# Graph attention and routed experts: normalising ahead of a mask conversion, and a score row made from a projection column

## The chip, the cores and the metric

The kernel runs on one core of a Trainium2 chip, in one launch. The metric is the device time of an execution in microseconds (us), as the median of several runs. The engines are named as the profile names them: PE is TensorE (PEld its weight load), DVE is VectorE, ACT is ScalarE, POOL is GpSimd, SP is SyncE, which here only issues transfers.

## The reference

```
x = x + gat(layernorm(x), adj)              # x is 4096 x 128, adj 4096 x 4096 of 0 and 1
x = x + ffn(layernorm(x))                   # eight experts, the best two for each row

gat(h, adj):  Wh = h @ W + b
              e[i, j] = leaky_relu(Wh[i] . a1 + Wh[j] . a2, 0.2), -9e15 where adj[i, j] is 0
              softmax over j, then attention @ Wh
ffn(x):       gate = x @ Wg.T + bg; top 2, softmax over the two
              out = sum over the two of p * (relu(x @ W1[e].T + b1[e]) @ W2[e].T + b2[e])
```

## The kernel before

Nodes are cut into 32 tiles of 128, and the tiles into 8 row groups of four (GT = 4). Attention is worked off in five stages of destination tiles, WB = [8, 8, 8, 6, 2], and each stage runs over all 32 source tiles. So there are 160 steps; step n = 32 g + u handles source tile u for stage g.

In a step, VectorE's `weigh(n)` (line 971) builds the weights of one source tile for all destinations of the stage, from three things: a row over destinations `c_bc` (128 equal partitions, one value for each destination), a column over sources `E_col`, and the mask `G`. It takes the larger of row and column and the smaller of that and the mask. TensorE's `attend(n)` (line 1600) multiplies `Wh` of the source tile with these weights and adds up in the two accumulators `acc`. The mask comes as int32 from DRAM in chunks of two steps (SP, `load_chunk`, line 531) and is converted to bf16 by ScalarE (`edges`, line 1355). At the end of a stage ScalarE's `evacuate` (line 1386) copies both accumulators to `numT`, and the rest of the stage's work (division, second layer norm, gate, routing) is spread over the steps of the next stage. The experts' tiles run between later steps and after them.

Each engine follows an order written out by hand: a loop over steps n in which each piece of work has its step, with ScalarE starting its conversions 6 steps ahead, VectorE its weights 4 steps ahead, and SP its loads 12 steps ahead. Engines wait for each other only by semaphores. `group_at(n, part, first)` says which row group i has its turn at step n: group i comes at n = 4 (i - 2) + part. `weigh` may be five steps ahead of `attend`, for there are six buffers `prob`.

The first stage also prepares the row groups i = 0 to 7. VectorE takes mean and variance (`stats`), GpSimd raises to the power -1/2 and makes the bias (`pow_group`, its last operation in line 702), ScalarE normalises four tiles (`normalise`, line 1320; groups 0 and 1 on VectorE), TensorE transposes them (`transposes`, line 1545), ScalarE copies the result out of PSUM (`keep_hT`, line 1329), TensorE projects them on the nine columns of `wag` (`project`, line 1558: the source score and eight gate columns), and ScalarE makes the column values (`keep_E`, lines 1336 and 1337). For the destinations' row, TensorE multiplies a matrix that holds the vector a1 in each column with the transposed group, a product of 512 columns (`project_s`, line 1567), and ScalarE takes the exponential into `c_bc` (`keep_s`, line 1347). Groups 0 to 3 have this in stage 0; groups 4 to 7 in stage 1, at steps 48, 50, 52 and 54 (`row_at`). VectorE cuts the row of each next stage off at 1 (`group_row`, line 940).

There is a second branch (`general`) for scores of a wide reach, which is not taken with these inputs.

Of the kernel before, what the change touches and what calls it, by code (L numbers as in the profile page):

```python
# [5 lines left out]
def build(nc, x, adjT, W, Wb, a, WgT, bg, wcat, wlast, b2, out):  # L6
    fp32, fp16, bf16 = mybir.dt.float32, mybir.dt.float16, mybir.dt.bfloat16
    i32, u32 = mybir.dt.int32, mybir.dt.uint32
    ALU = mybir.AluOpType
# [19 lines left out]
    GC = 1 + E  # L29
    TW = FW + E + 1  # L30
# [98 lines left out]
    with ctx:  # L129
# [10 lines left out]
        ybuf = nc.dram_tensor("ybuf", (2 * N, F), fp32).ap()  # L140

# [23 lines left out]
        def cut(base, *dims):  # L165
# [25 lines left out]
        wag = sb("wag", [P, GC])  # L191
# [34 lines left out]
            .rearrange("p (e f) -> p e f", f=F)  # L226
        rden = sb("rden", [P, SB])
# [79 lines left out]
        def row_at(n):  # L307

            i, r = divmod(n - TILES - 16, 2)
            return GT + i if r == 0 and 0 <= i < GROUPS - GT else None  # L310
# [13 lines left out]
        def score_row(i, late):  # L324

            return yt[:, i % 2, :] if late else acc[1][:, :] if i == 1 else m1[:, :]
# [13 lines left out]
        def projected_col(tiles, c):  # L340

            return pj[:, 0:TILES * GC].rearrange("p (u c) -> p u c", c=GC)[:, tiles, c]

# [42 lines left out]
        s_cg = sem("s_cg")  # L386
# [121 lines left out]
        def _(sp):  # L508
# [41 lines left out]

            rows, places = {}, {}
# [297 lines left out]
        def _(dve):  # L849
# [39 lines left out]
            def keep_Wh(i, general):  # L889
                tiles = slice(GT * i, GT * (i + 1))  # L890
                dve.wait_ge(s_ED, i + 1)
                if general:
                    nc.vector.tensor_copy(t_col[:, tiles], projected_col(tiles, 0))
# [17 lines left out]
            nc.vector.tensor_copy(wag[:, 0:1], wa[:, 1:2])  # L911
# [5 lines left out]
            nc.vector.tensor_tensor(wag[:, 1:GC], WgT_sb[:, :], wglast_bc[:, :], ALU.subtract).then_inc(s_wag, 1)  # L917
# [322 lines left out]
            def main(general):  # L1240
                for n in range(-LB, NS):
# [3 lines left out]
                    if not general:  # L1245
# [6 lines left out]
                        if n >= 0 and n % TILES == TILES - 8 and n // TILES + 1 < SG:  # L1252
                            group_row(n // TILES + 1)
# [6 lines left out]
                    if n == 26:  # L1260
# [3 lines left out]
                        nc.vector.tensor_tensor(xg[:, :, :], pj[:, 0:TILES * GC].rearrange("p (u c) -> p u c", c=GC)[:, :, 1:GC],  # L1264
# [51 lines left out]
        def _(act):  # L1316
# [7 lines left out]
            def keep_hT(i):  # L1324
                act.wait_ge(s_t0, i + 1)
                if i < GT:
                    ge(act, s_sm, i - 1)
# [4 lines left out]
            def keep_E(i):  # L1332
                tiles = slice(GT * i, GT * (i + 1))
                act.wait_ge(s_wh, i + 1)
                t = projected_col(tiles, 0)
# [4 lines left out]
            def keep_s(i, general):  # L1340
                act.wait_ge(s_sm, i + 1)
                row = score_row(i, i >= GT and not general)
# [180 lines left out]
            with act.Else():  # L1523
                keep_s(0, True)
                keep_s(1, True)
                for i in range(GROUPS):
                    if i >= 2:
                        keep_hT(i)
# [7 lines left out]
        def _(pe):  # L1536
# [11 lines left out]
            def project(i, general=False):  # L1548
# [7 lines left out]
                for b in range(GT):  # L1556
                    at = (GT * i + b) * GC
                    last = nc.tensor.matmul(pj[:, at:at + GC], hT_of(i)[:, b * P:(b + 1) * P], wag[:, :],  # L1558
# [3 lines left out]
            def project_s(i, late=False):  # L1562
# [271 lines left out]
```

## Time and profile before

| what | value |
| --- | --- |
| median of 3 runs | 413.72 us (413.57 to 413.85) |
| the profiled execution | 413.95 us, span 412.2 us |
| mean granted TensorE clock | 0.989 of full speed |
| PE busy | 383.2 us, 93% of the span |
| DVE busy | 295.3 us, 72% |
| ACT busy | 270.1 us, 66% |
| POOL busy | 204.3 us, 50% |
| attention products (line 1600) | 236.0 us of PE in 576 records, two for each f32 product |
| row products (line 1567) | 16 records, 6 in bank m, 2 in acc, 8 in yt |

The span goes from the first to the last instruction of the profiled execution; its own time is 1.75 us longer. Busy times of PE are modelled from pipelined records. Times of other engines are durations of their instructions.

### The profile page before, as it was taken

The numbers are of one execution on the slowest core, as the hardware profiler recorded it, in microseconds if no ns is written. First come the engines' busy times: TensorE is split into PE (matmuls) and PEld (weight loads), VectorE is DVE, ScalarE is ACT, GpSimd is POOL, SyncE is SP. The second block draws the span as 40 slices with busy tenths as digits, with TensorE's granted clock in tenths as the row PEclk, the third lists the DMA queues.
The fourth block names the chain that finished last, engine by engine and source line by source line (L and its number), as shares of the span: only waits on it lengthen the run. The fifth ranks groups of instructions, "written<-read, shape, count | busy, mean of one in ns | idle before, by whom it ended". The sixth has DMA issues, their size and how long they took to land.

```text
span 412.2 us, 8417 instructions
## 1 busy us (share of the span) xinstructions
PE 383.2 (93%) x2434; PEld 257.1 (62%) x2434; DVE 295.3 (72%) x819; ACT 270.1 (66%) x451; POOL 204.3 (50%) x247
## 2 busy tenths in 40 slices
PE   1899999999999999999999999999989999999960
PEld 1545555444444444444366667798879999999960
DVE  5998896989799979899988696268951692111173
ACT  1589879675878666892376975458646666676630
POOL 3283451100401874206763058789787777555560
PEclk9999999999999999999999999999999999999995
DMA  6999998969959999898676994576577777667795
GB/s 197 358 425 373 344 353 251 422 250 374 384 220 305 354 302 408 322 319 328 185 244 236 380 316 145 184 245 219 191 231 237 251 239 240 218 222 240 243 361 184
DMA packets 45610, 116.44 MB, mean 282 GB/s; under 512 B 7517, under 2 KB 19682, under 8 KB 38902
## 3 DMA queue, kind: packets, MB, share of 16 engines
q1 hardware_dynamic: 37062, 100.02, 68.0%
q0 software_dynamic: 4320, 8.47, 6.2%
q10 hardware_dynamic: 4176, 7.34, 5.9%
q8 instruction: 23, 0.38, 0.4%
q14 instruction: 29, 0.24, 0.2%
HBM read 84.57 MB, written 13.07 MB: 237 GB/s over the span
## 4 chain that ended last, share of the span: by engine, by line
PE 75%; DMA 8%; DVE 6%; issue 4%; SPq 3%; ACT 2%; POOL 2%; ACTq 0%; POOLq 0%; DVEq 0%
PE acc L1600 46%; PE acc L1702 10%; DMA adj<-adjT 3%; PE hps L1684 3%; PE hps L1686 3%; PE hps L1685 3%; PE yt L1702 3%; DVE prob L971 2%; PE yt L1645 2%; DMA ybuf<-wst,dest 1%; DMA adj<-ybuf 1%; PE pj L1721 1%; PE pj L1558 1%; SPq L547 1%; PE yt L1567 1%
## 5 line engine op out<-in xcount | busy, mean ns | idle before, releaser
L1600 PE MATMUL acc<-prob,Wh 128*128 128x512 f32 (+1 forms) x576 | 236.0, 550 | 3.8 <-DVE prob L971 2.7
L971 DVE SCALAR_TENSOR_TENSOR prob<-s_bc,E_col,G_all 128x1024 f32<-128x1024 f32 (+2 forms) x159 | 169.7, 1096 | 21.9 <-PE acc L1600 18.5
L1600 PEld LDWEIGHTS acc<-prob,Wh 128*128 128x128 f32 x576 | 103.5, 190 | 98.8 <-issue 84.2
L1355 ACT ACTIVATE G_all<-adj 128x2048 bf16<-128x2048 int32 (+1 forms) x67 | 119.0, 1800 | 22.7 <-DMA adj<-adjT 12.8
L784 POOL DMA_INDIRECT xbuf<-xr,slot x64 | 72.6, 1135 | 49.6 <-PE acc L1600 30.5
L800 POOL DMA_INDIRECT ybuf<-wst,dest x71 | 73.2, 1031 | 45.4 <-ACT wst L1438 25.0
L1702 PE MATMUL acc<-wall,prob 128*128 x368 | 51.1, 282 | 0.0
L1702 PEld LDWEIGHTS acc<-wall,prob 128*128 128x128 f32 x368 | 44.7, 192 | 0.2
L1223 DVE COPY share<-slab 128x1 f32<-128x1 f32 x45 | 6.8, 155 | 47.1 <-DMA slab<-xbuf 44.5
L1428 ACT ACTIVATE prob<-hps 128x512 f32<-128x512 f32 x46 | 27.6, 599 | 6.5 <-PE hps L1686 1.4
L1438 ACT ACTIVATE wst<-acc,share 128x128 f32<-128x128 f32 x45 | 16.6, 368 | 17.3 <-PE acc L1702 15.6
L708 POOL TENSOR_TENSOR wst<-wst,wlb 127x512 f32<-127x512 f32 x8 | 13.5, 1685 | 28.2 <-DMA wlb<-wlast 28.2
L766 POOL TENSOR_TENSOR rstd<-ve,mhalf 128x8 f32<-128x8 f32 x3 | 5.0, 1660 | 45.2 <-DVE ve L1073 45.2
L1702 PE MATMUL yt<-wall,wst 128*128 x192 | 26.8, 282 | 0.0
L1702 PEld LDWEIGHTS yt<-wall,wst 128*128 128x128 f32 x192 | 23.3, 192 | 4.2 <-issue 2.3
L694 POOL TENSOR_TENSOR scratch<-scratch,mhalf 128x4 f32<-128x4 f32 x8 | 13.1, 1634 | 23.4 <-DVE scratch L876 23.4
L1686 PE MATMUL hps<-prob,s_bc 128*128 128x128 f16 x124 | 22.4, 219 | 0.0
L1685 PE MATMUL hps<-prob,s_bc 128*128 128x128 f16 x124 | 22.4, 219 | 0.0
L1684 PE MATMUL hps<-prob,s_bc 128*128 128x128 f16 x124 | 22.4, 219 | 0.0
L1438 ACT ACTIVATE wst<-yt,slab 128x128 f32<-128x128 f32 x24 | 8.8, 368 | 17.0 <-PE yt L1702 16.1
L1645 PE MATMUL yt<-ident,slab 128*128 128x128 f16 x142 | 19.5, 219 | 0.0
L1428 ACT ACTIVATE wst<-hps 128x512 f32<-128x512 f32 x25 | 14.9, 598 | 5.5 <-PE hps L1686 5.4
(249 smaller groups left out, 554.0 us busy)
## 6 DMA issues: line engine op xcount, KB each, us to landing
adj<-adjT SPq DMA_DIRECT2D x52, 1024.0 KB, 8.1
adj<-adjT SPq DMA_DIRECT2D x16, 768.0 KB, 6.2
s_bc<-wall SPq DMA_DIRECT2D x47, 256.0 KB
wlb<-wall SPq DMA_DIRECT2D x24, 256.0 KB
slab<-xbuf SPq DMA_DIRECT2D x71, 65.0 KB
adj<-ybuf SPq DMA_DIRECT2D x6, 512.0 KB, 7.7
xs<-x SPq DMA_DIRECT2D x8, 256.0 KB, 10.5
wst<-wcat ACTq DMA_DIRECT2D x8, 256.0 KB, 4.2
```

The source lines that it names most:

```text
L784: nc.gpsimd.indirect_dma_start(xbuf[:, :], bass.IndirectOffsetOnAxis(ap=slot[:, w, b:b + 1].bitcast(u32), axis=0), xr[:, w, b, :], None).t ...
L800: nc.gpsimd.indirect_dma_start(ybuf[:, :], bass.IndirectOffsetOnAxis(ap=dest[:, t:t + 1].bitcast(u32), axis=0), ysb[t % YR][:, :], None, b ...
L971: nc.vector.scalar_tensor_tensor(prob[n % PR][:, 0:w], c_bc[:, P * AT[g]:P * AT[g] + w], E_col[:, u:u + 1], G[m % GR][:, k * w:(k + 1) * w ...
L1355: nc.scalar.activation(G[m % GR][:, 0:w], adj_sb[m % AR][:, 0:w], ACT.Relu).then_inc(s_G, 1)
L1428: nc.scalar.activation(hid_of(t), hps[t % 2][:, :], ACT.Relu).then_inc(s_hh, 1)
L1438: nc.scalar.activation(ysb[t % YR][:, :], yps_of(t), ACT.Copy, scale=part).then_inc(s_ye, 1)
L1600: last = nc.tensor.matmul(bank[:, 0:k * P], Wh[:, u, :], prob[n % PR][:, b * P:(b + k) * P], start=(u == 0), stop=(u == TILES - 1), skip_g ...
L1645: last = nc.tensor.transpose(tps_of(t)[:, h * P:(h + 1) * P], x16[:, h * P:(h + 1) * P], ident16[:, :])
L1684: nc.tensor.matmul(dst, whi, xhi, start=(k == 0), stop=False, skip_group_check=True)
L1685: nc.tensor.matmul(dst, whi, xlo, start=False, stop=False, skip_group_check=True)
L1686: last = nc.tensor.matmul(dst, wlo, xhi, start=False, stop=True, skip_group_check=True)
L1702: last = nc.tensor.matmul(yps, hid_of(t)[:, j * P:(j + 1) * P], weights(t, UW + 2 * j * P, 2 * P).bitcast(fp32), start=False, stop=(j == K ...
```

## The change

On ScalarE, `normalise(i)` of groups 3 to 7 moves one step ahead, from n = 4 (i - 2) - 1 to n = 4 (i - 2) - 2. In a step, normalising stands first, then `keep_hT`, and `edges` behind both.

The destination scores of groups 2 to 7 are no longer made by a product of 512 columns. `wag` gets a tenth column with a1, so that `project` gives each node's destination score as a column value. Tiles 8 to 15 are run 0, tiles 16 to 31 run 1. For each run, ScalarE takes the exponential of the column (`make_run`, steps 8 and 24), TensorE transposes it to rows (`turn_run`, steps 11 and 27), VectorE cuts it off at 1 into a part of `numT` (`keep_run`, steps 12 and 28), SP stores the 8 or 16 rows of 128 values in a DRAM tensor `cbuf` (`send_run`, its steps 16 and 32) and loads it into all 128 partitions of `c_bc` (`spread_run`, its steps 22 and 38). `weigh` waits for that load at the first step of a stage that uses it. `group_row`, `row_at` and the six row products go. New waits: ScalarE waits for the store of run 1 before it evacuates stage 0; TensorE waits for `keep_run` before it writes the shared bank `yt` at steps 20 and 30.

```diff
+    PC = 2 + E
+        cbuf = nc.dram_tensor("cbuf", (1, N), fp32).ap()
-        wag = sb("wag", [P, GC])
+        wag = sb("wag", [P, PC])
+        c_col = sb("c_col", [P, TILES])
+        c_rows = numT[:, E * F // 2:E * F // 2 + P]
...
+        runs = [range(2 * GT, 4 * GT), range(4 * GT, TILES)]
+        def run_at(n, part):
+            last = [8, 24]
+            return last.index(n - part) if n - part in last else None
+        def turned(r):
+            return yt[0:len(runs[r]), 0, 2 * P:3 * P]
+        def run_words(r):
+            return slice(runs[r].start * P, runs[r].stop * P)
...
+            def send_run(r):
+                sp.wait_ge(s_cr, r + 1)
+                sp.dma_start(cbuf[0:1, run_words(r)].rearrange("a (u p) -> (a u) p", p=P),
+                             c_rows[0:len(runs[r]), :]).then_inc(s_cw[r], 16)
+            def spread_run(r):
+                sp.wait_ge(s_cw[r], 16)
+                sp.dma_start(c_bc[:, run_words(r)],
+                             cbuf[0:1, run_words(r)].broadcast_to([P, len(runs[r]) * P])).then_inc(s_cb[r], 16)
...
+                    if not general:
+                        r = run_at(n, 8)
+                        if r is not None:
+                            send_run(r)
+                        r = run_at(n, 14)
+                        if r is not None:
+                            spread_run(r)
...
-            nc.vector.tensor_copy(wag[:, 0:1], wa[:, 1:2])
+            nc.vector.tensor_copy(wag[:, 0:2], wa[:, 0:2])
...
-            def group_row(g):
-                dve.wait_ge(s_sbc, (AT[g] + WB[g] + GT - 1) // GT)
-                c = c_bc[:, P * AT[g]:P * (AT[g] + WB[g])]
-                nc.vector.tensor_scalar(c, c, 1.0, None, ALU.min).then_inc(s_cg, 1)
+            def keep_run(r):
+                dve.wait_ge(s_ct, r + 1)
+                if r:
+                    dve.wait_ge(s_cw[r - 1], 16)
+                nc.vector.tensor_scalar(c_rows[0:len(runs[r]), :], turned(r), 1.0, None, ALU.min).then_inc(s_cr, 1)
...
-                if u == 0 and g:
-                    dve.wait_ge(s_cg, g)
+                if u == 0:
+                    for r, tiles in enumerate(runs):
+                        if tiles.start < AT[g] + WB[g] and AT[g] < tiles.stop:
+                            dve.wait_ge(s_cb[r], 16)
...
-                    ge(act, s_sm, i - 1)
+                    ge(act, s_sm, i - 1 if general else min(i - 1, 2))
...
+            def make_run(r):
+                mine = runs[r]
+                act.wait_ge(s_wh, mine.stop // GT)
+                nc.scalar.activation(c_col[:, mine.start:mine.stop], projected_col(slice(mine.start, mine.stop), 0), ACT.Exp,
+                                     bias=bC[:, :], scale=-(1.0 - SLOPE)).then_inc(s_cc, 1)
...
+                    if n == TILES and not general:
+                        act.wait_ge(s_cw[-1], 16)
                     if 0 < n <= STEPS and n % TILES == 0:
                         evacuate(n // TILES - 1)
...
-                        i = 2 if n == -1 else group_at(n, -1, 3)
+                        i = 2 if n == -1 else group_at(n, -2, 3)
                         if i is not None:
                             normalise(i)
...
-                            if i < GT:
-                                keep_s(i, general)
-                        i = row_at(n)
-                        if i is not None:
-                            keep_s(i, general)
+                        r = run_at(n, 0)
+                        if r is not None:
+                            make_run(r)
...
+            def turn_run(r):
+                pe.wait_ge(s_cc, r + 1)
+                if r:
+                    pe.wait_ge(s_wgc, 1)
+                nc.tensor.transpose(turned(r), c_col[:, runs[r].start:runs[r].stop], ident[:, :]).then_inc(s_ct, 1)
...
                     if n == 20:
+                        if not general:
+                            pe.wait_ge(s_cr, 1)
                         gate_weights()
                     if n == 30:
+                        if not general:
+                            pe.wait_ge(s_cr, len(runs))
...
-                            if i < GT:
-                                project_s(i)
-                        i = row_at(n)
-                        if i is not None:
-                            project_s(i, True)
+                        r = run_at(n, 3)
+                        if r is not None:
+                            turn_run(r)
```

## Rows read from the trace of the kernel before

**Rows 1.** Windows over stages: stretch, length, busy us of each engine, PEclk, DMA share, GB/s

```profile
32.00:206.00 174.00, 172.80 (x488) 81.61 (x487) 157.93 (x294) 126.05 (x158) 59.74 (x55) 1.00 0.90 323
70.00:86.00 16.00, 16.00 (x42) 7.20 (x41) 15.93 (x23) 9.03 (x8) 1.98 (x3) 1.00 0.98 402
```

**Rows 2.** Chain that ended last, in order of time: start, us, what

```profile
36.39 0.96 PE m L1567 x2
...
115.84 0.86 PE yt L1567 x2
116.69 3.43 PE acc L1600 x8
...
128.93 0.96 PE yt L1567 x2
```

**Rows 3.** Timeline of TensorE, stage 0: start, us, line, operation, idle before and releaser

```profile
26.20 1.06 PE L1558 MATMUL pj<-wag,xnT 128*128 128x9 f32 x8
...
31.51 0.66 PE L1545 MATMUL hps<-ident,Wh 128*128 128x128 f32 x4 [1.57 <-ACT Wh L1320]
...
35.44 0.95 PE L1558 MATMUL pj<-wag,xnT 128*128 128x9 f32 x8
...
60.90 0.95 PE L1558 MATMUL pj<-wag,wall 128*128 128x9 f32 x8
...
63.51 0.27 PE L1746 MATMUL yt<-ident,Wx 128*128 128x128 f32 x1
```

**Rows 4.** Timeline of ScalarE, stage 0 and the border to stage 1

```profile
28.01 1.91 ACT L1355 ACTIVATE G_all<-adj 128x2048 bf16<-128x2048 int32 x1 [1.86 <-DMA adj<-adjT]
29.83 0.86 ACT L1320 ACTIVATE Wh<-xs,nm,scratch 128x127 f32<-128x127 f32 x2
...
58.63 0.60 ACT L1329 ACTIVATE wall<-hps 128x512 f32<-128x512 f32 x1 [0.72 <-issue]
59.13 0.19 ACT L1329 ACTIVATION_READ_ACCUMULATOR wall<-hps 128x1 f32 x1
...
85.42 1.46 ACT L1386 ACTIVATE numT<-acc,lost 128x512 f32<-128x512 f32 x2 [5.01 <-PE acc L1600]
```

**Rows 5.** Timeline of GpSimd, last operation of group 3's statistics

```profile
25.77 1.12 POOL L702 TENSOR_TENSOR nm<-zero,nm 128x4 f32<-128x4 f32 x1
```

**Rows 6.** Timeline of VectorE, end of stage 0

```profile
74.82 0.68 DVE L940 TENSOR_SCALAR s_bc<-s_bc 128x1024 f32<-128x1024 f32 x1
...
79.34 4.86 DVE L971 SCALAR_TENSOR_TENSOR prob<-s_bc,E_col,G_all 128x1024 f32<-128x1024 f32 x4
```

**Rows 7.** Line 531 at 77 to 78 us (ns; landing), whole run, DMA issues (KB, us to landing)

```profile
L531 SPq DMA_DIRECT2D adj<-adjT x1: 328/328/328, 77.5 to 77.5; - x1
DMA to landing us min/median/max: 8.4/8.4/8.4
...
DMA to landing us min/median/max: 4.1/7.2/14.1
...
out<-xs SPq DMA_DIRECT2D x2, 64.0 KB, 2.0
...
bg_bc<-bg SPq DMA_DIRECT2D x1, 4.0 KB, 10.5
```

**Rows 8.** Windows of 2 us around the border

```profile
66.00:68.00 2.00, 2.00 (x7) 0.95 (x6) 1.97 (x2) 2.00 (x4) 0.00 (x0) 1.00 0.46 142
86.00:88.00 2.00, 1.91 (x5) 0.86 (x5) 2.00 (x3) 1.91 (x3) 0.00 (x0) 1.00 0.18 74
```

**Rows 9.** Timelines of ScalarE, VectorE and TensorE, 157 to 198 us

```profile
157.79 1.91 ACT L1355 ACTIVATE G_all<-adj 128x2048 bf16<-128x2048 int32 x1 [4.61 <-DMA adj<-adjT]
...
168.32 1.65 ACT L1401 ACTIVATE xn<-xs,xnT,rstd 128x128 f32<-128x128 f32 x4 [1.38 <-POOL xnT L768]
...
171.80 1.28 DVE L971 SCALAR_TENSOR_TENSOR prob<-s_bc,E_col,G_all 128x1024 f32<-128x1024 f32 x1 [0.56 <-ACT G_all L1355]
...
196.88 1.55 PE L1600 MATMUL acc<-prob,Wh 128*128 128x512 f32 x3 [0.96 <-DVE prob L971]
```

More of the change, by code:

```diff
@@ L305, in hT_of @@
             return wall[:, E - 2 + (i - GT) // 2, (i % 2) * 2 * GW:(i % 2 + 1) * 2 * GW].bitcast(fp32)
-        def row_at(n):
-            i, r = divmod(n - TILES - 16, 2)
-            return GT + i if r == 0 and 0 <= i < GROUPS - GT else None
+        runs = [range(2 * GT, 4 * GT), range(4 * GT, TILES)]
[6 more added lines that the diff above has]
+            return slice(runs[r].start * P, runs[r].stop * P)
         def hid_of(t):
@@ L322, in tps_of, with score_row @@
             return tps[1 if t <= TAIL + 1 else (t + TAIL + 1) % 2]
-        def score_row(i, late):
-            return yt[:, i % 2, :] if late else acc[1][:, :] if i == 1 else m1[:, :]
+        def score_row(i):
+            return acc[1][:, :] if i == 1 else m1[:, :]
         def halves(g):
@@ L340, in projected_col @@
         def projected_col(tiles, c):
-            return pj[:, 0:TILES * GC].rearrange("p (u c) -> p u c", c=GC)[:, tiles, c]
+            return pj[:, 0:TILES * PC].rearrange("p (u c) -> p u c", c=PC)[:, tiles, c]
         s_wa = sem("s_wa")
@@ L385, in build @@
         s_whs = sem("s_whs")
-        s_cg = sem("s_cg")
+        s_cc = sem("s_cc")
+        s_ct = sem("s_ct")
+        s_cr = sem("s_cr")
+        s_cw = [sem(f"s_cw{i}") for i in range(len(runs))]
+        s_cb = [sem(f"s_cb{i}") for i in range(len(runs))]
         s_hs = sem("s_hs")
@@ L892, in keep_Wh @@
                 if general:
-                    nc.vector.tensor_copy(t_col[:, tiles], projected_col(tiles, 0))
+                    nc.vector.tensor_copy(t_col[:, tiles], projected_col(tiles, 1))
                 nc.vector.tensor_tensor(Wh[:, tiles, :], Wh[:, tiles, :],
@@ L916, in _ @@
             dve.wait_ge(s_we, 32)
-            nc.vector.tensor_tensor(wag[:, 1:GC], WgT_sb[:, :], wglast_bc[:, :], ALU.subtract).then_inc(s_wag, 1)
+            nc.vector.tensor_tensor(wag[:, 2:PC], WgT_sb[:, :], wglast_bc[:, :], ALU.subtract).then_inc(s_wag, 1)
             dve.wait_ge(s_tq, 1)
@@ L1251, in main @@
                             keep_Wh(i, False)
-                        if n >= 0 and n % TILES == TILES - 8 and n // TILES + 1 < SG:
-                            group_row(n // TILES + 1)
+                        r = run_at(n, 4)
+                        if r is not None:
+                            keep_run(r)
                     e = expert_at(n, 4)
@@ L1263, in main @@
                         link(nc.vector.tensor_tensor(sig0[:, :], ve0[:, :], rs0[:, :], ALU.mult))
[L1264 removed]
+                        nc.vector.tensor_tensor(xg[:, :, :], pj[:, 0:TILES * PC].rearrange("p (u c) -> p u c", c=PC)[:, :, 2:PC],
                                                 sig0[:, :].unsqueeze(2).broadcast_to([P, TILES, E]),
@@ L1322, in normalise, with keep_hT @@
                 ins.then_inc(s_xh, 1)
-            def keep_hT(i):
+            def keep_hT(i, general=False):
                 act.wait_ge(s_t0, i + 1)
                 if i < GT:
-                    ge(act, s_sm, i - 1)
+                    ge(act, s_sm, i - 1 if general else min(i - 1, 2))
                     ge(act, s_wh, i - 1)
@@ L1334, in keep_E @@
                 act.wait_ge(s_wh, i + 1)
-                t = projected_col(tiles, 0)
+                t = projected_col(tiles, 1)
                 nc.scalar.activation(w_col[:, tiles], t, ACT.Exp, bias=bD[:, :], scale=dsc[:, :])
@@ L1341, in keep_s @@
                 act.wait_ge(s_sm, i + 1)
-                row = score_row(i, i >= GT and not general)
+                row = score_row(i)
                 if general:
@@ L1527, in _ @@
                     if i >= 2:
-                        keep_hT(i)
+                        keep_hT(i, True)
                     keep_E(i)
@@ L1556, in project, with project_s @@
                 for b in range(GT):
-                    at = (GT * i + b) * GC
-                    last = nc.tensor.matmul(pj[:, at:at + GC], hT_of(i)[:, b * P:(b + 1) * P], wag[:, :],
+                    at = (GT * i + b) * PC
+                    last = nc.tensor.matmul(pj[:, at:at + PC], hT_of(i)[:, b * P:(b + 1) * P], wag[:, :],
                                             start=True, stop=True)
                 last.then_inc(s_wh, 1)
-            def project_s(i, late=False):
+            def project_s(i):
                 pe.wait_ge(s_hT, i + 1)
                 if i >= 2:
-                    pe.wait_ge(s_sbc, i - 1 if late and i > GT else i)
-                row = score_row(i, late)
-                nc.tensor.matmul(row, wa1_bc[:, :], hT_of(i), start=True, stop=True).then_inc(s_sm, 1)
+                    pe.wait_ge(s_sbc, i)
+                nc.tensor.matmul(score_row(i), wa1_bc[:, :], hT_of(i), start=True, stop=True).then_inc(s_sm, 1)
             pe.wait_ge(s_WTs, 1)
@@ L1718, in through @@
                 if g == 0 and q == 1:
-                    pe.wait_ge(s_sbc, GT)
+                    pe.wait_ge(s_sbc, 2)
                 for b in thirds(g)[q]:
@@ L1769, in main @@
                             project(i)
-                            if i < GT:
-                                project_s(i)
-                        i = row_at(n)
-                        if i is not None:
-                            project_s(i, True)
+                        r = run_at(n, 3)
+                        if r is not None:
+                            turn_run(r)
                     if n >= STEPS:
@@ L1791, in _ @@
                     project_s(i)
+                pe.wait_ge(s_sbc, GROUPS)
                 main(True)
```

1 line of the change is left out of this document (removed).

## The prediction

> **What bounds the kernel now.** I read the windows by stage first, then the chain of waits, then the timelines of TensorE and of the engines that release it. From 32 to 206 us TensorE is busy for 172.80 of 174 us [rows 1]: a matmul taken out of this stretch is worth its own duration, unless something else becomes late. VectorE is close behind it in places, 15.93 of 16 us from 70 to 86 [rows 1]. One step of the weighted sum over eight tiles is two f32 products; two steps take 3.43 us on the chain [rows 2], so one takes 1.72. In stage 0 TensorE has one stall of size, 1.57 us before the transposes of row group 3 at 31.51 [rows 3]. Its releaser is ScalarE's normalise(3), which began at 29.83 because the mask conversion ahead of it began at 28.01, after 1.86 us of waiting for its chunk [rows 4]. Group 3's statistics were ready at 26.89, the end of GpSimd's last operation for it (25.77 + 1.12) [rows 5]. The change puts normalise(3) ahead of that conversion.
>
> **Part 1, stage 0 (steps 0 to 31).** Two row products go, project_s(2) and (3), 0.96 us each [rows 2], and the stall of 1.57. But as ScalarE's order is now written, normalise(i+1) stands in the same step as keep_hT(i) and ahead of it. At step 2 it waits until 26.89 and takes some 1.65 us (29.83 to the 31.51 at which it let TensorE go) [rows 3, 4]. So keep_hT(2), which let project(2) start at 26.20 [rows 3], starts at 28.5, takes the 0.6 and 0.1 to 0.2 of the pair at 58.63 [rows 4] and lets project(2) start at 29.25. TensorE stands still for 3.05 us where it ran before. Sum to step 7: +3.05 - 0.96 - 0.96 - 1.57 = -0.44. The mask conversion moves from 28.01 to 29.25 and ends near 31.2; its first step, 8, comes on TensorE after project(3), which ran at 35.44 [rows 3], so it is covered. Groups 4 and 5 are normalised before their transposes are there: no stall. Group 6 is tight. keep_hT(6) began at 58.63, right behind three DMA issues [rows 4]; with normalise(7) ahead of it, it begins near 60.3 and ends near 61.0, or up to 0.4 sooner if the issues come sooner, and project(6), at 60.90 before [rows 3], is wanted at 60.5. This gives 0.1 to 0.4 back. The two transposes of the new column cost 0.1 each, between 0 and the 0.27 of the nearest record [rows 3]. TensorE ends step 31 some 0.2 us earlier; bounds 0.5 later and 3.5 earlier (project(2) not held up).
>
> **Part 2, the border to stage 1.** ScalarE must now wait, before it evacuates stage 0's accumulators into numT, until the second run of the score row (16 rows of 512 bytes that lie in numT) has landed in DRAM. Behind the wait stands evacuate(0), and behind that step 32. Evacuation began at 85.42, after 5.01 us of idle time [rows 4]. When does the store land? keep_run(1) stands on VectorE after the weights of step 32. The four from 79.34 (steps 31 to 34, 4.86 us) [rows 6] bring step 32's to 81.8; the clip of 0.68 us at 74.82 [rows 6], in the same gapless stretch, goes: 81.1. With about 0.2 for the new clip (between 0 and 0.68) and 0.33 for the issue [rows 7] the store enters SP's queue at 81.6. Ahead of it lies the chunk issued at 77.5, which landed 8.4 us later, at 85.9 [rows 7], in a stretch where transfers are 0.98 busy [rows 1]. A 4 KB load behind a full queue took 10.5 us, a 64 KB store on an empty one 2.0, and the adjacency loads between 4.1 and 14.1 [rows 7]. So the landing lies between 83.6 and 95.7. I take the full queue, which is nearest: 85.9, and 0.2 to 0.4 more for the first spread, whose 512 KB take 1.3 us at 402 GB/s [rows 1], of which the idle 1.08 us between 66 and 68 hide most [rows 8]. At 86.3, evacuation and step 32 come 0.9 us later than before, and the 0.2 of part 1 are lost in the same wait.
>
> The Trainium skill, page DMA: Bandwidth & Descriptors, section Queues, rings and completion order, says that each DMA engine takes a ring's descriptors in order and that the semaphore increment lands only after that engine's earlier writes. By that the store does wait for the chunk, and the sum stays as it is; the 10.5 us of a 4 KB load agree. Its section Anatomy of one DMA puts most of a fixed 2 us into the write's receipt; by that alone the store would land at 83.6 and the sum would be the one of rival A.
>
> SP stands still here from about 80.5 to 81.2 for keep_run(1); behind it is the next chunk's load. Transfers ran dry at 86 (0.18 busy from 86 to 88 [rows 8]), so a microsecond is covered; without that cover it would cost that microsecond. The first spread is asked for near 63, when step 18's conversion ends, and wanted near 79.9; at the worst load's 14.1 it is there.
>
> **Part 3, stage 1 (steps 32 to 63).** Four row products go, of 0.86 (three) and 0.96 us on the chain from 115.84 to 128.93 [rows 2]; without the change-over in the last that is 3.44, on an engine that is busy throughout. ScalarE loses four waits for them and four exponentials, so it converts chunks and asks for new ones earlier. The second spread, 1 MB near 91 us, takes 2.6 us of transfers at 402 GB/s [rows 1]; VectorE may be five steps (8.6 us) ahead of TensorE, as its six buffers allow, which covers it; uncovered it would cost its 2.6.
>
> **Costed at nothing.** The two small exponentials, each under the 0.60 of a 128x512 copy [rows 4], run while ScalarE is ahead; uncovered they cost up to 1.2. The tenth column and the wider copy of wag add one column to each. The four row clips leave VectorE where TensorE sets the pace, so beyond part 2 they gain nothing, or up to 0.5 near 198 us.
>
> **Part 4, passing it on.** After 147 us ScalarE waited 4.61 us for a chunk at 157.79, VectorE is gapless from 171.80, and TensorE waits 0.96 for it at 196.88 [rows 9]. If that chunk came no earlier, the conversion at 157.79 would start the same chain, and only the waits inside it would be saved: 1.38 at 168.32 [rows 9], so some 1.4 us would pass. But the chunk is asked for by earlier conversions, which no longer wait for TensorE's rows, so I take the whole shift to pass. Later stages follow TensorE's steps and move as a whole.
>
> **Sum.** The profiled execution took 413.95 us, 412.2 of it the span. +0.9 - 3.44 = -2.54, so 411.4; against the median of 413.72, 0.23 lower, 411.2.
>
> **Rivals.** (A) The store lands before evacuation wants it. For it speak the 2.0 us on an empty queue, against it the full one. Then 0.3 at most from part 1 and 3.44 remain: 410.0. (B) Slower: the store lands late. It decides from 85.42 + 3.44 + 0.83 = 89.7, 8.1 us after its issue; the chunk ahead needed 8.4 from its own issue, the worst 14.1, which would give 95.7, 10.3 - 3.44 = 6.8 us more than before, 420.6. Against it: of that queue only some two chunks lie ahead. (C) Late chunks after 147 us swallow a part: 1.5 of the gain or less stays, 412.2 to 413.3. For it speaks the wait of 4.61, against it the earlier requests. (D) project(2) isn't held up, should GpSimd's rough spans show the statistics too late, and the store is early as well: 3.5 and 3.44 go, 406.8. That nothing is saved by the rows would need an idle TensorE near 116 us; it isn't.
>
> **Chances.** Forecast 0.50, A 0.20, B 0.07, C 0.18, D 0.05. About 0.2%, 0.83 us, is what a measurement of this kernel can tell from no change; of C 0.08 lie within it, of the forecast 0.01. The forecast's own range is 410.5 to 412.0; the range over the cases reaches beyond A below and to C's end above, 409.3 to 413.1. Faster 0.84, same 0.09, slower 0.07.
>
> **What would show it.** In the profile after: project(2) near 29.3 behind some 3 us of waiting for ScalarE, no stall before the transposes of group 3, and step 7 about 0.4 us earlier; an evacuation near 86.3 released by a DMA, with about 0.9 us of idle TensorE more ahead of step 32; no row products between 110 and 130, and stage 2 begun 2.5 us earlier; the wait near 196 no larger than 0.96. Wrong would make it a store that lands at another time, a stall of a microsecond before one of project(3) to (7), or a larger wait near 194.

## The result: the changed kernel is slower

| | before | after |
|---|---|---|
| median of 19 executions each, us | 413.69 | 416.84 |
| lowest to highest, us | 412.51 to 415.73 | 412.99 to 419.46 |
| profiled execution, own time and span, us | 413.95, 412.2 | 415.37, 413.6 |

The ratio of after to before is 1.0061, with a 95% interval of 1.0042 to 1.0080. Medians here and below are of all executions; the ratios leave out those that lie over 1.5% above the fastest of the same kernel, among them one of 1396.44 us in e3. The forecast of 411.2 us, its range of 409.3 to 413.1 and its sign are all missed.

The windows of after, first three of stage 0, then the long stretch of [rows 1] (columns as there; the third number from the end is PEclk, the granted clock of TensorE):

```profile
30.00:32.00 2.00, 2.00 (x7) 1.04 (x8) 1.26 (x2) 2.00 (x4) 1.92 (x7) 0.82 0.98 387
32.00:34.00 2.00, 2.00 (x7) 1.22 (x6) 2.00 (x3) 1.79 (x3) 1.31 (x2) 0.50 1.00 369
34.00:36.00 2.00, 2.00 (x5) 0.89 (x4) 1.93 (x11) 2.00 (x6) 0.00 (x0) 0.82 0.90 330
...
32.00:206.00 174.00, 170.62 (x484) 80.73 (x482) 157.62 (x293) 122.06 (x154) 61.35 (x56) 0.99 0.90 333
```

From 32 to 206 us TensorE is busy for 2.18 us less than in [rows 1], yet the last evacuation in that stretch, evacuate(2), doesn't come sooner (205.13 us, before 204.97). And between 30 and 36 us its clock isn't always the full 2.4 GHz; from 32 to 34 it is 0.50, 1.2 GHz. At 0.50 the three windows come to some 3.4 us, (0.18 + 0.50 + 0.18) x 2 us / 0.5. The timeline of TensorE in after, stage 0, answers [rows 3]:

```profile
29.27 1.06 PE L1607 MATMUL pj<-wag,xnT 128*128 128x10 f32 x8 [3.00 <-ACT xnT L1371]
30.18 2.68 PE L1655 MATMUL acc<-prob,Wh 128*128 128x512 f32 x4
32.66 1.06 PE L1594 MATMUL hps<-ident,Wh 128*128 128x128 f32 x4
33.51 4.20 PE L1655 MATMUL acc<-prob,Wh 128*128 128x512 f32 x8
37.55 0.95 PE L1607 MATMUL pj<-wag,xnT 128*128 128x10 f32 x8
```

The stall of project(2) and its place are as forecast: 3.00 us, to 29.27. What follows is not. Four transposes took 1.06 us here and 0.66 in [rows 3]. ScalarE in the same stretch (answers the first half of [rows 4]):

```profile
27.00 1.64 ACT L1362 ACTIVATE Wh<-xs,nm,scratch 128x127 f32<-128x127 f32 x4 [1.36 <-POOL nm L739]
28.55 0.57 ACT L1371 ACTIVATE xnT<-hps 128x512 f32<-128x512 f32 x1
```

At the border to stage 1 the chain of waits of after reads:

```profile
82.24 0.20 DVE numT L979
...
82.46 4.70 DMA cbuf<-numT
...
87.18 0.70 ACT numT L1435
...
88.01 4.10 PE acc L1655 x9
```

The store was in flight for 4.70 us, as forecast (81.6 to 86.3), and was the last thing that evacuate(0) waited for, but it was issued 0.86 us later than forecast. That follows stage 0: the store is issued 63.45 us behind project(1) in after, 62.10 where the clock doesn't fall (e6 below) and 60.62 where the stall is gone as well (e3). Evacuate(0) stands at 87.18 against 85.42 [rows 4], 1.76 later.

Then stage 1. The four row products are gone, but at step 64, where stage 2 begins, TensorE stands still. Timelines of VectorE, GpSimd, ScalarE and TensorE in after, 135 to 148 us:

```profile
135.65 0.17 DVE L1169 CAST slot<-slotf 128x16 int32<-128x16 f32 x1
...
136.85 1.25 POOL L821 DMA_INDIRECT xbuf<-xr,slot  x1 [6.83 <-PE acc L1655]
138.41 1.83 POOL L821 DMA_INDIRECT xbuf<-xr,slot  x1 [0.30 <-issue]
140.54 1.50 POOL L821 DMA_INDIRECT xbuf<-xr,slot  x1 [0.30 <-PE acc L1655]
142.35 2.08 POOL L821 DMA_INDIRECT xbuf<-xr,slot  x1 [0.32 <-PE acc L1655]
144.45 1.46 POOL L745 TENSOR_TENSOR wst<-wst,wlb 127x512 f32<-127x512 f32 x1
...
145.94 0.63 ACT L1414 ACTIVATE wall<-wst 128x512 f16<-128x512 f32 x1 [4.84 <-POOL wst L745]
146.48 1.25 ACT L1435 ACTIVATE numT<-acc,lost 128x512 f32<-128x512 f32 x2
...
147.29 3.24 PE L1655 MATMUL acc<-prob,Wh 128*128 128x512 f32 x7 [1.89 <-ACT numT L1435]
```

Read it upwards. TensorE waits for evacuate(1) (L1435). That stands on ScalarE behind the high weights of the last expert (L1414), which waited 4.84 us for GpSimd's shift of those weights (L745). The shift stands on GpSimd behind four sends (L821), and the first send needs VectorE's slot numbers (L1169). Evacuate(1) began with no wait of its own, so what set it was this chain and not TensorE. The same places in the kernel before, on VectorE, GpSimd and ScalarE (L1128 makes the slot numbers, L784 are the sends, L708 the shift, L1386 evacuates):

```profile
133.34 0.17 DVE L1128 CAST slot<-slotf 128x16 int32<-128x16 f32 x1
...
134.54 1.25 POOL L784 DMA_INDIRECT xbuf<-xr,slot  x1 [5.70 <-issue]
...
140.35 1.47 POOL L708 TENSOR_TENSOR wst<-wst,wlb 127x512 f32<-127x512 f32 x1
...
146.30 1.49 ACT L1386 ACTIVATE numT<-acc,lost 128x512 f32<-128x512 f32 x2 [2.13 <-PE acc L1600]
```

There the shift was done at 141.82, 4.5 us ahead of evacuate(1), which waited for TensorE. Counted from evacuate(0), the shift ended 56.40 us behind it before and 58.73 in after: the slot numbers came 0.55 us later by that count, and from the first send to the shift it took 7.60 us instead of 5.81. From evacuate(1) to evacuate(2) this execution of after runs like before: evacuate(2) is at 205.13, before at 204.97.

### The profile page after: what moved, and what is told of

Read it like the earlier page. It is cut to its first block, busy times and chain, and to the rows that moved or that the text cites. A ratio compares the mean times of both kernels' runs of the same rounds, so it can differ in the third digit from the quotient of the medians.

```text
span 413.6 us, 8393 instructions
## 1 busy us (share of the span) xinstructions
PE 380.0 (92%) x2424; PEld 255.8 (62%) x2424; DVE 294.6 (71%) x817; ACT 266.8 (65%) x447; POOL 205.6 (50%) x247
## 4 chain that ended last, share of the span: by engine, by line
PE 62%; DVE 9%; DMA 8%; ACT 8%; issue 5%; SPq 3%; POOL 3%; ACTq 0%; POOLq 0%; DVEq 0%
PE acc L1655 33%; PE acc L1756 9%; PE yt L1756 4%; DVE prob L1012 4%; ACT G_all L1404 3%; PE hps L1738 3%; PE hps L1739 3%; PE hps L1740 3%; PE yt L1699 2%; DMA xbuf<-xr,slot 2%; DMA ybuf<-wst,dest 1%; DMA slab<-xbuf 1%; DMA adj<-ybuf 1%; DMA cbuf<-numT 1%; PE pj L1607 1%
## 5 line engine op out<-in xcount | busy, mean ns | idle before, releaser
L821 POOL DMA_INDIRECT xbuf<-xr,slot x64 | 75.0, 1172 | 46.2 <-PE acc L1655 31.7
L745 POOL TENSOR_TENSOR wst<-wst,wlb 127x512 f32<-127x512 f32 x8 | 12.4, 1554 | 35.0 <-DMA wlb<-wlast 34.9
L803 POOL TENSOR_TENSOR rstd<-ve,mhalf 128x8 f32<-128x8 f32 x3 | 5.0, 1660 | 39.8 <-DVE ve L1114 39.8
L1699 PEld LDWEIGHTS yt<-ident,slab 128*128 128x128 f16 x142 | 13.6, 98 | 8.5 <-issue 5.1
```

The source lines that it names most:

```text
L821: nc.gpsimd.indirect_dma_start(xbuf[:, :], bass.IndirectOffsetOnAxis(ap=slot[:, w, b:b + 1].bitcast(u32), axis=0), xr[:, w, b, :], None).t ...
L1699: last = nc.tensor.transpose(tps_of(t)[:, h * P:(h + 1) * P], x16[:, h * P:(h + 1) * P], ident16[:, :])
```

## The experiments

Theory 1: the order of ScalarE starves TensorE at project(2), its clock falls behind the stall, and what is left of the gain is swallowed where TensorE waits for ScalarE. Theory 2, the rival: the spread's two transfers per score row slow the rest of the kernel. (Some of the expectations call the evacuations "combine passes" and the score rows "capacity rows".)

Beginnings (us) read from the timelines of TensorE and ScalarE of the profiled executions, E0 to E2 being the three evacuations; the last columns are the median of 7 to 19 executions and the ratio to the kernel before on the same chip:

| kernel | project(1) | (2) | (3) | E0 | E1 | E2 | median | ratio |
|---|---|---|---|---|---|---|---|---|
| before | 18.92 | 26.20 | 35.44 | 85.42 | 146.30 | 204.97 | 413.69 | |
| after | 19.01 | 29.27 | 37.55 | 87.18 | 146.48 | 205.13 | 416.84 | 1.0061 |
| after again (e8) | 20.40 | 30.67 | 38.95 | 88.21 | 147.52 | 207.87 | 417.07 | 1.0055 |
| e1 order alone | 18.93 | 29.20 | 38.34 | 88.32 | 149.20 | 207.86 | 418.54 | 1.0099 |
| e2 rows alone | 20.73 | 27.99 | 35.26 | 86.19 | 144.32 | 206.08 | 415.56 | 1.0018 |
| e3 copy first | 18.82 | 26.08 | 33.09 | 84.49 | 143.69 | 202.34 | 414.37 | 1.0015 |
| e6 filler | 20.69 | 30.77 | 37.36 | 87.55 | 146.78 | 206.84 | 413.82 | 0.9983 |
| e4 own tile too | 20.70 | 27.96 | 34.85 | 85.85 | 145.16 | 205.51 | 412.79 | 0.9966 |
| e7 own tile alone | 20.69 | 30.96 | 39.24 | 88.50 | 147.80 | 209.49 | 415.36 | 1.0017 |
| e5 experts sooner | 20.70 | 27.96 | 34.97 | 85.88 | 143.33 | 205.13 | 414.24 | 0.9997 |
| e9 statistics sooner | 18.73 | 26.21 | 32.99 | 82.52 | 140.02 | 198.70 | 410.47 | 0.9936 |
| e10 copy first on before | 20.80 | 28.05 | 35.63 | 85.72 | 146.60 | 205.27 | 413.23 | 0.9982 |
| e11 after, passed on | 18.50 | 28.77 | 37.05 | 86.74 | 144.18 | 202.85 | 413.39 | 0.9995 |

Project(1) is at 18.5 to 19.0 in some profiled executions and at 20.4 to 20.8 in others, whatever the edit (after shows both). So the table is read by distances between columns, and the median beside them. Distances of single executions vary too: e5 and e9 have the same code up to E0, and from project(1) to E0 they take 65.18 and 63.79 us. The profiled executions of e4, e6 and e7 took 416.85, 416.26 and 420.50 us, well above their medians, that of e3 411.34, well below.

**e1, the order alone.** The kernel before, with nothing but ScalarE's normalise one step sooner:

```
-  i = 2 if n == -1 else group_at(n, -1, 3)
+  i = 2 if n == -1 else group_at(n, -2, 3)
   ...normalise(i), then keep_hT, as before
```

> The kernel before with only normalise(i) one step ahead. Theory 1 (the order starves TensorE and its clock pays): project(2) near 29.3 behind about 3 us of waiting, granted clock below 1.0 in some window between 30 and 36 us, step 7 about 2.5 to 3 us later than before's 37.35, time about 415.5 to 416.5. Theory 2 (the new transfers are what costs, the order is harmless): the stall of 1.57 us before the transposes of group 3 is gone, time 412 to 413.7.

418.54 us, ratio 1.0099 (1.0062 to 1.0136). TensorE and a window of e1:

```profile
29.20 1.06 PE L1558 MATMUL pj<-wag,xnT 128*128 128x9 f32 x8 [3.01 <-ACT xnT L1329]
...
32.00:34.00 2.00, 2.00 (x4) 0.75 (x3) 2.00 (x3) 2.00 (x2) 1.24 (x2) 0.50 0.90 324
```

No spread is in this kernel, and it has the stall, the fallen clock, and a loss at least of the size of the whole change's (the intervals of the two ratios overlap). The time is above the 415.5 to 416.5 us that theory 1 expected. Its evacuations come 2.90, 2.90 and 2.89 us later than before: what stage 0 loses passes to stage 2 whole. The order alone makes the kernel slower.

**e2, the rows alone.** The changed kernel with the normalise where it was (`group_at(n, -1, 3)`).

> The changed kernel with normalise(i) back in its old step. Theory 1: project(2) back near 26.2, granted clock 1.0 throughout stage 0, step 7 about 1 us earlier than before; step 32 held to 86.5 to 87.3 by the store; stage 1's 3.4 us swallowed up to step 64 by the chain VectorE's slots, GpSimd's sends, the last expert's weights, evacuate(1); time 413 to 414.3, within 0.2% of before. Theory 2: 1.5 MB more of transfers slow the chunks whatever ScalarE's order, time 415.5 to 417.

415.56 us, ratio 1.0018 (0.9986 to 1.0050). Project(2) comes 7.26 us behind project(1), as before, and nothing is lost in stage 0. Yet the version is not below the kernel before: the stall is not the only thing that eats the gain. The time doesn't decide between the theories: the ratio is within the 0.2% of theory 1, the 415.56 us lie in the range of theory 2. E0 to E1 is 58.13 us, 2.75 less than before, and the chain at step 64 still holds E1 (TensorE waits 0.71 us there). E1 to E2 is 61.76, 3.09 more, in part behind this wait for VectorE, where the clock fell too (timeline of TensorE and a window of e2):

```profile
196.29 11.93 PE L1655 MATMUL acc<-prob,Wh 128*128 128x512 f32 x23 [2.13 <-DVE prob L1012]
...
198.00:200.00 2.00, 2.00 (x4) 0.90 (x3) 2.00 (x3) 1.28 (x1) 0.77 (x1) 0.50 0.58 114
```

**e6, filler.** The changed kernel with three products of 512 columns, which nobody reads, put on TensorE into the stall ahead of project(2):

```
+  if i == 2:
+      pe.wait_ge(s_sbc, 2)
+      for _ in range(3):
+          nc.tensor.matmul(m1[:, :], wa1_bc[:, :], hT_of(1), start=True, stop=True)
   if i is not None:
       project(i)
```

> The changed kernel with three products of 512 columns (nothing reads their result) that fill TensorE's wait before project(2). If the granted clock falls because TensorE stood idle, it stays 1.0 from 30 to 36 us, project(2) starts at the same time within 0.3 us, step 7 starts at 36.7 to 37.2 instead of 38.35, and the time is 0.5 to 1.4 us under that of the changed kernel. If the clock fell for another reason (the bursts after the stall), it falls here too, and step 7 stays near 38.3.

413.82 us, ratio 0.9983 (0.9956 to 1.0010). TensorE and a window of e6:

```profile
27.79 2.74 PE L1829 MATMUL m<-xnT,scratch 128*128 128x512 f32 x6
30.77 1.06 PE L1607 MATMUL pj<-wag,xnT 128*128 128x10 f32 x8 [0.25 <-ACT xnT L1371]
...
33.49 0.60 PE L1594 MATMUL hps<-ident,Wh 128*128 128x128 f32 x4
...
32.00:34.00 2.00, 2.00 (x9) 1.03 (x8) 1.25 (x3) 2.00 (x4) 1.84 (x4) 1.00 0.81 226
```

Project(2) is still held up, but the clock stays at 1.00, and from project(2) to project(3) it takes 6.59 us instead of 8.28. So the clock behind the stall cost 1.69 us, on top of the stall's own 3.00. Useless work made the changed kernel faster by more than that, about 3 us by the ratios of 0.9983 and 1.0061, whose intervals don't meet; the rest of it isn't traced. In the profile itself, 1.31 of the 1.69 us are left at E0, counted from project(1), and E1 to E2 takes 60.06 us, 1.41 more than in after.

**e3, copy first.** The changed kernel with ScalarE's order keep_hT, normalise, masks:

```
+  i = group_at(n, 2)
+  if i is not None:
+      keep_hT(i)
   i = 2 if n == -1 else group_at(n, -2, 3)
   if i is not None:
       normalise(i)
-  i = group_at(n, 2)
-  if i is not None:
-      keep_hT(i)
```

> The changed kernel with the order keep_hT(i), normalise(i+1), edges in a step. Theory 1: neither stall of stage 0 is left (project(2) near 26.2, transposes of group 3 near 28.8), clock 1.0, step 7 1 to 3.5 us earlier than before's 37.35; the store still holds step 32; time 411.5 to 413.3. Theory 2: 415 to 417, for the spreads are still there.

414.37 us, ratio 1.0015 (0.9988 to 1.0042). Project(2) comes 7.26 us behind project(1) and project(3) 7.01 behind it, clock 1.00: the whole stall is gone. The time lies between the ranges of the two theories. But at the border the store is what comes last now, and the clock falls there instead (ScalarE, TensorE and a window of e3):

```profile
84.49 1.27 ACT L1435 ACTIVATE numT<-acc,lost 128x512 f32<-128x512 f32 x2 [5.72 <-DMA cbuf<-numT]
...
85.33 7.08 PE L1655 MATMUL acc<-prob,Wh 128*128 128x512 f32 x12 [1.93 <-ACT numT L1435]
...
86.00:88.00 2.00, 2.00 (x4) 0.97 (x3) 0.07 (x1) 2.00 (x2) 0.00 (x0) 0.50 0.06 25
```

The same twelve matmuls took 5.39 us in after, 7.08 here: 1.69 us again.

**e4, copy first and a tile of its own.** As e3, with the second run's rows in a tile that evacuate(0) doesn't write, so that it waits for the first run's store alone:

```
-  c_rows = numT[:, E * F // 2:E * F // 2 + P]
+  c_rows = [numT[:, E * F // 2:E * F // 2 + P], wlast_bc]
...
-  act.wait_ge(s_cw[-1], 16)
+  act.wait_ge(s_cw[0], 16)
```

> As the version with ScalarE's copy first, but the second run's capacity rows lie in a tile of their own, so that ScalarE's first combine pass waits for the first run's store alone. Theory 1 (ScalarE's order starves TensorE, its granted clock falls, and what is left of the gain is swallowed where TensorE waits for ScalarE): project(2) near 26.1 us at clock 1.00; the first combine pass near 83 us with no wait of TensorE over 0.5 us and a clock of 1.00 in 84 to 90 us; 410 to 413 us. Theory 2 (the spread's two transfers per row slow the rest of the kernel): the transfers are the same, so the time stays near 414 us however early step 32 begins.

412.79 us, ratio 0.9966 (0.9943 to 0.9988): faster than the kernel before, with the same transfers as after. Theory 2, by which the time stays near 414 us, falls here; what the transfers cost by themselves was not measured. Evacuate(0) waits for TensorE and no longer for the store.

**e7, the tile alone**, in the changed kernel.

> The changed kernel with nothing but the tile of its own for the second run's capacity rows. Theory 1: project(2) still waits 3.0 us and the clock still falls to about 0.5 behind it; step 32 comes 0.5 to 1 us sooner than in the changed kernel, and step 64, which waits for the last expert's high weights, where it was: 415 to 417 us, within 0.3% of the changed kernel. If the store at the border were what made the change slower, the time would come to 412 to 413 us.

415.36 us, ratio 1.0017 (0.9993 to 1.0041). Project(2) is 10.27 us behind project(1), the stall 3.01. The interval overlaps that of e8 on the same chip, so this doesn't settle whether the store costs the changed kernel anything. In e8 evacuate(0) waited for TensorE even without this edit, and E0 is 67.81 us behind project(1) in both, so in this pair the tile moved nothing at the border.

**e8, the changed kernel again.**

> The changed kernel itself, once more, beside the others on one chip, to see how far its time and its profile repeat. Every theory: a median of 415 to 418 us, 0.3 to 0.9% over the kernel before; project(2) near 29.3 us behind a wait of 3.0 us with a clock of about 0.5 after it, or, if the profiled execution starts late at project(1) as two of the other versions did, the same distance from project(1) to project(2) of 10.3 us.

417.07 us (412.71 to 420.29), ratio 1.0055 (1.0026 to 1.0083). Project(1) to project(2) is 10.27 us, in after 10.26. It also showed something new at step 64 (TensorE and a window of e8):

```profile
148.33 7.08 PE L1655 MATMUL acc<-prob,Wh 128*128 128x512 f32 x12 [1.89 <-ACT numT L1435]
...
150.00:152.00 2.00, 2.00 (x3) 0.68 (x2) 1.46 (x2) 2.00 (x2) 1.62 (x2) 0.50 0.98 363
```

The wait is the 1.89 us of after, but here the clock fell behind it, and the step took 7.08 us; in after it took 5.39 at a clock of 1.00:

```profile
147.29 5.39 PE L1655 MATMUL acc<-prob,Wh 128*128 128x512 f32 x12 [1.89 <-ACT numT L1435]
```

**e5, experts sooner.** As e4, with the preparation of experts 4 to 7 (load, shift, high and low weights) five steps sooner, so that the last shift is ahead of the sends:

```
-  ... else divmod(n - part - TILES + 7, 5)
+  ... else divmod(n - part - TILES + 12, 5)
```

> As the version with copy first and own tile, and the preparation of experts 4 to 7 stands five steps sooner in stage 1. Theory 1, second half (the four products saved in stage 1 are swallowed at step 64, because the chain from VectorE's slot numbers over GpSimd's sends and the last expert's shift holds ScalarE's high weights and so its combine pass): the last high weights of ScalarE end before 143 us, the second combine pass begins with TensorE and not with them, and step 64 comes 1 to 2.5 us sooner than without this edit; 1 to 2 us less in time. Rival (the combine pass waits for something else as late, the transfers or ScalarE's own work): step 64 within 0.5 us of the version without it, and the same time.

E1 now waits for TensorE and comes 57.45 us behind E0, in e4 59.31. So the chain at step 64 was real, and it took 1.86 us. But 414.24 us, ratio 0.9997 (0.9973 to 1.0022): the time did not follow (the interval overlaps that of e4), so the theory was right on step 64 and missed the end. E1 to E2 is 61.80 us, and the chain moved on. GpSimd, ScalarE, VectorE and TensorE of e5:

```profile
164.25 1.42 POOL L821 DMA_INDIRECT xbuf<-xr,slot  x1 [0.30 <-issue]
165.69 2.40 POOL L803 TENSOR_TENSOR rstd<-ve,mhalf 128x8 f32<-128x8 f32 x1
...
168.47 1.65 ACT L1450 ACTIVATE xn<-xs,xnT,rstd 128x128 f32<-128x128 f32 x4 [4.51 <-POOL xnT L805]
...
171.95 1.29 DVE L1012 SCALAR_TENSOR_TENSOR prob<-s_bc,E_col,G_all 128x1024 f32<-128x1024 f32 x1 [3.68 <-ACT G_all L1404]
...
180.67 0.20 PE L1790 MATMUL m<-M,upper 128*128 128x64 bf16 x1 [1.78 <-DVE M L1147]
...
197.04 3.27 PE L1655 MATMUL acc<-prob,Wh 128*128 128x512 f32 x7 [2.14 <-DVE prob L1012]
```

GpSimd sends its sixteen blocks one after another, 0.30 us apart, from 135.58 to 165.67. Its statistics of row group 1 (L803) stand behind the last, and ScalarE, VectorE and TensorE wait for them in turn. So the send queue, which begins with VectorE's slot numbers, sets this stretch. The same hold stands in e2, e6 and e7, whose statistics also begin right behind the sixteenth send and take 2.40 or 2.41 us; there too TensorE waits 2.13 or 2.14 us for prob. In after, e3, e4 and e8 they begin 1.05 us behind the last send and take 1.67, and the wait is 0.95 or 0.96.

**e9, the statistics sooner.** As e5, with those statistics ahead of the last two sends:

```
-  if calm(g) and p == 8:
+  if calm(g) and g != 1 and p == 8:
       pow_rows(g)
...
+  if n == 2 * TILES + 6:
+      pow_rows(1)
   ...shift_weights, then the sends of step n
```

> As the version with copy first, own tile and experts sooner, and GpSimd's statistics for row group 1 stand ahead of its last two sends instead of behind the sixteenth. Theory (GpSimd's sixteen sends, 0.30 us apart from 135.6 to 165.7 us, are the next thing that swallows the gain: its statistics end at 168.4 us and hold ScalarE's normalise, the mask copies behind it, VectorE's routing and TensorE's count products at 180.7 us with a wait of 1.8 us): the statistics end near 165.2 us, the wait for the mask at the count products goes, the third combine pass begins 1.5 to 2.5 us sooner than the 205.1 us of the version without this edit, and the time is 1 to 2.5 us less, 411 to 413 us. Rival (VectorE's own row products bound the second half of stage 2, where TensorE waited 2.1 us for prob at 197.0 us): the count products come sooner, but the third combine pass stays within 0.5 us of 205.1 us and the time at 414 us.

410.47 us, ratio 0.9936 (0.9909 to 0.9963), the fastest of all and below both kernels, and below the 411 to 413 us expected. ScalarE's evacuations in e9, each waiting for TensorE:

```profile
82.52 1.46 ACT L1437 ACTIVATE numT<-acc,lost 128x512 f32<-128x512 f32 x2 [4.37 <-PE acc L1657]
...
140.02 1.49 ACT L1437 ACTIVATE numT<-acc,lost 128x512 f32<-128x512 f32 x2 [4.08 <-PE acc L1657]
...
198.70 1.49 ACT L1437 ACTIVATE numT<-acc,lost 128x512 f32<-128x512 f32 x2 [4.17 <-PE acc L1657]
```

E1 to E2 is 58.68 us, as before (58.67), and the gain of 2.90, 6.28 and 6.27 us at the three evacuations holds. The wait for prob near the end of stage 2 is back to 0.96, that of [rows 9].

**e11, the changed kernel, passed on.** Nothing but the two edits of e5 and e9 in the changed kernel; its order, stall and store are its own.

> The changed kernel with its own order of ScalarE and its own tiles, and only the two chokes behind stage 1 taken away: experts 4 to 7 prepared five steps sooner, and the statistics of row group 1 ahead of the last two sends. Theory: stage 0 loses its 1.3 us as in the changed kernel (project(2) behind a wait of 3.0 us, clock near 0.5 after it), but the four products saved in stage 1 reach the end: the second and third combine passes 1.5 to 2.5 us sooner than in the changed kernel, 413.5 to 415.5 us, about as the kernel before. Rival (what makes the changed kernel slower lies elsewhere, in the transfers): within 0.2% of the changed kernel, 416 to 417 us.

413.39 us, ratio 0.9995 (0.9974 to 1.0016). The stall at project(2) is 2.94 us and the clock behind it low, as in after, but E0 to E1 is 57.44 and E1 to E2 58.67: the four products reach the end of stage 2.

**e10, copy first on the kernel before**, all its row products kept.

> The kernel before with ScalarE's order of the copy-first version alone: copy of the transposed rows, then the normalise one step sooner, then the masks; all row products of stages 1 and 2 as before. Theory 1: project(2) near 26 to 26.2 us and TensorE gains back its 1.6 us wait at 31.5 us, clock 1.00 throughout stage 0, step 32 about 1 to 1.5 us sooner, and with no choke in stage 1 most of it reaches the end: 412 to 413.5 us, 0.2 to 0.5% below the kernel before. If the order itself is worth nothing even without the stall, it is within 0.1% of the kernel before; if any normalise ahead of the masks costs, it is slower.

413.23 us, ratio 0.9982 (0.9961 to 1.0003): the time is in the expected range, but the interval includes 1, so a gain isn't shown by it. Project(2) comes 7.25 us behind project(1) and project(3) 7.58 behind it, 9.24 before, so the 1.57 us wait of [rows 3] is gone. From project(1) to E0 it takes 64.92 us, before 66.50. The 1.58 us are about that wait, but one pair of profiles doesn't price the edit: e5 and e9, with the same code there, differ by 1.39.

## Why the prediction was wrong

**Part 1, the stall: place and length right, price wrong.** Project(2) stood at 29.27 (forecast 29.25) after 3.00 us (3.05), and the wait ahead of group 3's transposes went. The sum took a stall to cost its own length and the rows' durations of before to hold behind it. But TensorE came out of the stall at half its clock, and e6 puts that at 1.69 us. On the chain of waits attention step 7 began at 38.50; the forecast had it 0.44 us sooner than the 37.35 of before, so at 36.91. The clock's 1.69 accounts for that miss of 1.59. The stall's price is the first failed step.

The Trainium skill, page TensorE: Matmul & The Clock Gate, section Part 1: The HAM clock gate (the "warmup" mystery), says that throttled is the clock's default state, released by activity, and that the window over which activity is judged runs free of the kernel. The traces agree as far as they go: the clock fell behind stalls and in e6, where the stall was filled, nowhere; and the wait of 1.89 us at step 64 brought it down in e8 and not in after, which a window of its own timing allows. The window itself no run here shows.

**Part 2, the border: duration right, start wrong.** The store took 4.70 us, as forecast, and landed at 87.16. The DMA engines were busy for 0.97 or more of each microsecond from 82 to 87 and for 0.53 of the next, so it did land behind a full queue and not after the 2.0 us of an empty one. That it waited for the chunk right ahead of it, issued at 77.8, isn't shown, for the profile has no landing of that chunk; the chunk before that, issued at 76.0, took 8.5 us. The whole excess, 1.76 us later instead of 0.9, is the later issue, inherited from part 1.

**Part 3, the rows: right.** Where nothing held E1 (e5, e9, e11), E0 to E1 fell from 60.88 us to 57.45, 57.50 and 57.44, by 3.38 to 3.44, against the 3.44 of the sum.

**Part 4, passing it on: the second failed step.** I looked for what could swallow the gain after 147 us only; there the profiled execution of after lost nothing (E1 to E2 58.65, before 58.67). The gain was swallowed just ahead, at step 64: E0 to E1 in after is 59.30, so 1.58 of 3.44 us passed. The prediction took the whole shift to pass and never followed the queue of GpSimd up to step 64. With the chain of before, evacuate(1) could have begun at E0 + 56.97 (the shift's end, and 0.57 to E1 as in after), below the 57.45 that TensorE needs: 3.44 would just have fitted. But the chain grew by 2.33 us with the change. In the three profiles with row products (before, e1, e10) the first four sends took 4.87 to 4.88 us together, in after 6.66, in e2 5.52. That other work of VectorE now runs beside these sends is a possible link; it wasn't tested.

The three together at E2: -2.54 as forecast, +0.86 from the border, +1.86 from step 64, is +0.18; measured +0.16.

**The rivals.** The store landed neither early nor late (A, B), and project(2) was held up (D). C had a part of the gain swallowed, but by late chunks after 147 us, and gave 412.2 to 413.3. No rival had the loss where the profile of after has it, and none had a stall cost more than its length.

**What stays open.** From E2 to the end of the span after takes 1.2 us more than before, but e8, the same kernel, 1.1 less than after (207.3 and 208.5), and e9 209.7, so this part varies by itself and I put no cause to it. And the medians differ by 3.15 us, the two profiled executions by 1.42, so the profile of after doesn't hold the whole loss. Two things that it lacks are seen in other profiles with the same chain at step 64. The clock fell there behind 1.89 or 1.90 us of waiting in e8 and e4 (1.69 us in e8), and not behind 1.84 to 1.90 us in after, e6 and e7. And in e6 and e7 GpSimd's statistics stood right behind the last send, and E1 to E2 took 60.06 and 61.69 us. Either could add to the median; that they do, and how often they happen, was not measured. The e11 run, where that wait is gone, spans 411.42 to 415.38, after again 412.71 to 420.29.

## What to carry to other kernels

A stall of TensorE is priced by its length and by the slower clock behind it: here 3.00 us of waiting cost 4.69, while no fall followed the 1.57 us stall that it replaced, so an edit that makes a longer stall out of a shorter one can lose more than the difference. Time taken off an engine reaches the end only if the next thing it waits for has slack; at the first hand-over behind the edit, follow the queues of the engines that hand over up to the producer that the edit doesn't move (here VectorE's slot numbers and GpSimd's sends). In an in-order queue, put first what the bounding engine wants first: the copy ahead of the normalise, the statistics ahead of the last sends.

## What the hardware showed that I had not expected

The granted clock fell to 0.50 behind every stall of 2.94 to 3.01 us ahead of project(2) (after, e1, e7, e8, e11), and behind some waits of 1.9 to 2.1 us: behind 1.93 at the border in e3, 1.89 and 1.90 at step 64 in e8 and e4, 2.13 and 2.14 near 196 to 200 us in e2 and e7. It didn't fall behind 1.57 in before, behind 1.84 to 1.90 at step 64 in after, e6 and e7, or behind 2.13 and 2.14 near 197 to 199 us in e6 and e5. So at these lengths the wait alone doesn't decide. The three falls that can be priced (project(2), the border in e3, step 64 in e8) cost 1.69 us each.

There was also slowness that the granted clock doesn't show. Project(0) and the matmuls behind it, first in after, then in e8:

```profile
13.97 1.09 PE L1607 MATMUL pj<-wag,xnT 128*128 128x10 f32 x8
...
16.64 1.13 PE L1655 MATMUL acc<-prob,Wh 128*128 128x512 f32 x2 [0.62 <-DVE prob L993]
```

```profile
13.80 1.72 PE L1607 MATMUL pj<-wag,xnT 128*128 128x10 f32 x8
...
17.21 1.96 PE L1655 MATMUL acc<-prob,Wh 128*128 128x512 f32 x2
...
16.00:18.00 2.00, 2.00 (x3) 0.50 (x2) 0.95 (x2) 0.61 (x2) 0.00 (x0) 1.00 0.99 386
```

The same instructions took 1.6 to 1.7 times as long with a granted clock of 1.00 on record. Project(0) took 1.72 us in all seven profiles with the later project(1) and 0.96 to 1.09 in the six others, the kernel before among them, so that is where the later project(1) comes from. Both kinds are there for the same kernel (after and e8), and it is why positions were compared by distances.

GpSimd's sends took 0.95 to 2.10 us each for the same instruction, and the first four took 4.87 to 4.88 us together in every profile with row products; what makes them slower without isn't settled.
